# A transformer kernel with a mixture of experts on one core: the way the experts' results are sent, loaded, added and stored at the end of the program

## The reference

```
xn = layernorm(x)
x  = x + attention0(xn) + dense_ffn(xn)          # layer 0
xn = layernorm(x)
x  = x + attention1(xn) @ Wo.T + bo + moe(xn)    # layer 1, masked in blocks of 64

moe: probs = softmax(xf @ gate_w.T); top 2 of 8 experts, weights w normalised
     a token keeps its place at an expert while its rank there is < 320
     out = sum over e of comb[:, e] * (silu(xf@g_e) * (xf@u_e)) @ d_e
```

## Time and profile before

| what | us |
|---|---|
| median of 3 runs (530.13 to 531.07) | 530.15 |
| the profiled execution, its own time | 527.27 |
| its span, first to last instruction | 524.9 |
| PE busy of it | 452.6 |
| DVE busy of it | 400.5 |
| ACT busy of it | 330.0 |
| POOL busy of it | 262.3 |

### The profile page before, as it was taken

How to read it: one execution, slowest core, us unless ns; L and a number is a source line. 1 busy time by engine, 2 the same in 40 slices (tenths; PEclk the granted TensorE clock), 3 DMA queues, 4 the chain that set the end, 5 groups by cost and what they waited for, 6 DMA issues and landing times.

```text
span 524.9 us, 9470 instructions
## 1 busy us (share of the span) xinstructions
PE 452.6 (86%) x3442; PEld 175.6 (33%) x3442; DVE 400.5 (76%) x562; ACT 330.0 (63%) x434; POOL 262.3 (50%) x499
## 2 busy tenths in 40 slices
PE   3555989999999999999989888988999999999850
PEld 1201123324332443244324322321345545455510
DVE  4599889986998699969986987898887777633204
ACT  2201677775777677866785777767856665767550
POOL 6781075723535383788377757873202323253250
PEclk9855899999999999999999999999999999999995
DMA  3896439525720361545263635464720111010018
GB/s 85 232 235 101 76 125 262 173 113 175 148 105 2 124 64 19 64 145 61 24 71 121 79 34 68 142 76 63 88 65 29 46 44 51 11 43 25 16 61 213
DMA packets 143742, 48.27 MB, mean 92 GB/s; under 512 B 109890, under 2 KB 139090, under 8 KB 142866
## 3 DMA queue, kind: packets, MB, share of 16 engines
q1 hardware_dynamic: 141394, 42.93, 39.2%
q0 software_dynamic: 2304, 4.76, 2.7%
HBM read 22.81 MB, written 23.14 MB: 88 GB/s over the span
## 4 chain that ended last, share of the span: by engine, by line
PE 52%; DVE 18%; issue 9%; ACT 9%; SPq 6%; DMA 4%; POOL 1%; POOLq 0%; ACTq 0%; DVEq 0%
PE ps L779 13%; DVE mx L1147 12%; PE ps L763 9%; PE ps L748 7%; ACT PT L992 5%; SPq L446 4%; PE ps L828 4%; PE ps L820 3%; PE ps L709 2%; PE ps L821 2%; PE ps L803 2%; PE ps L843 2%; PE ps L840 2%; PE ps L804 2%; DMA h_all<-y_tokens 1%
## 5 line engine op out<-in xcount | busy, mean ns | idle before, releaser
L1147 DVE TENSOR_REDUCE mx<-ps 128x2 f32<-128x1024 f32 x256 | 307.6, 1221 | 58.6 <-PE ps L748 55.1
L992 ACT ACTIVATE PT<-ps 128x1024 f32<-128x1024 f32 x256 | 258.8, 1025 | 108.2 <-PE ps L763 101.7
L779 PE MATMUL ps<-PT,Vp 128*32 128x512 f32 x1024 | 137.2, 608 | 4.5 <-ACT PT L992 4.4
L748 PE MATMUL ps<-KO,QO 48*128 48x512 bf16 (+1 forms) x512 | 103.9, 404 | 33.8 <-ACT PT L992 15.7
L763 PE MATMUL ps<-QO,KO 59*128 59x512 bf16 x512 | 99.8, 388 | 1.8 <-DVE mx L1147 1.7
L536 POOL DMA_INDIRECT y_tokens<-expert_io,meta x40 | 38.5, 963 | 70.9 <-ACT expert_io L1027 48.1
L763 PEld LDWEIGHTS ps<-QO,KO 59*128 59x128 bf16 x512 | 24.5, 93 | 137.9 <-issue 74.6
L1169 DVE SCALAR_TENSOR_TENSOR th<-th,ps 128x320 f32<-128x320 f32 (+1 forms) x56 | 25.5, 455 | 32.0 <-ACT th L1012 31.6
L748 PEld LDWEIGHTS ps<-KO,QO 48*128 48x128 bf16 (+1 forms) x512 | 25.5, 95 | 63.5 <-ACT PT L992 29.6
L525 POOL DMA_INDIRECT x_places<-xe,place_i x32 | 31.9, 996 | 20.4 <-ACT PT L992 14.6
L561 POOL CAST mp<-mx 128x32 bf16<-128x32 f32 x16 | 3.4, 213 | 72.9 <-DVE mx L1147 69.0
(11 more groups left out here) (166 smaller groups left out, 485.9 us busy)
## 6 DMA issues: line engine op xcount, KB each, us to landing
z<-part SPq DMA_DIRECT2D x16, 384.0 KB, 2.6
z<-part SPq DMA_DIRECT2D x16, 256.0 KB, 3.0
QO<-z SPq DMA_DIRECT2D x64, 48.0 KB
KO<-z SPq DMA_DIRECT2D x64, 48.0 KB
x_places<-expert_io SPq DMA_DIRECT2D x2, 1300.0 KB, 7.2
expert_io<-x_places SPq DMA_DIRECT2D x8, 320.0 KB, 3.7
QO<-z SPq DMA_DIRECT2D x6, 384.0 KB
KO<-z SPq DMA_DIRECT2D x6, 384.0 KB
```

The lines of the kernel that those rows point to most:

```text
L748: mm = pe.matmul(ps[:, 2 * pair + half, :], rows_of(QO[u % 3], half, 2 * s + jj, rows, (qt, qt + 1)), rows_of(KO[u % 3], half, 2 * s + jj, ...
L779: last = pe.matmul(ps[32 * g:32 * g + 32, PV_BANK, :], Vp[u % 2][:, k, head(s, g), :], PT[:, (2 * t + g % 2) % 4, g // 2, :], start=(s % 2 ...
L992: act.activation(PT[:, e % 4], ps[:, 2 * pair:2 * pair + 2, :], ACT.Exp).then_inc(exp_done, 1)
L1147: dve.tensor_reduce(mx[:, a, qt, col:col + 5:4], ps[:, 2 * pair:2 * pair + 2, :], AX_X, ALU.max, negate=True).then_inc(max_read, 1)
```

## The change

Five things are edited. `send_results` keeps its waits on the exponentials only for experts 0 to 2. The rows of `y_tokens` within a sequence are numbered p * 4 + t in place of t * 128 + p (`dest_0`), so that a partition's four tokens are 2 KB in a row. The loads are one pair for each sequence (eight of 256 KB), issued and stored in the order 0, 2, 1, 3 (`ARRIVALS`), each sequence with semaphores of its own. GpSimd adds the results of sequences 0 and 1, behind its last send; VectorE those of 2 and 3, and the projection of unit 7 after them. The last copy into `o_T` is made in two halves, of tiles 0 and 1 and of tiles 2 and 3, and the last projection goes to PV_BANK, tiles 0 and 1 after the first half.

```diff
@@ -234,9 +234,9 @@
         expert_ps = sem("expert_ps")
         y_copied = sem("y_copied")
         y_sent = [sem(f"y_sent{i}") for i in range(2)]
-        y_in = [sem(f"y_in{i}") for i in range(2)]
-        first_added = sem("first_added")
-        result = sem("result")
+        y_in = [sem(f"y_in{b}") for b in range(B)]
+        first_added = [sem(f"first_added{b}") for b in range(B)]
+        result = [sem(f"result{b}") for b in range(B)]
         logit_ps = sem("logit_ps")
         lg_max = sem("lg_max")
         lg_ready = sem("lg_ready")
@@ -376,24 +376,27 @@
             for e in range(E):
                 sp.dma_start(meta[:, e], src[:, e, :, D:ROW]).then_inc(meta_in, 16)
 
-        def results_of(pair):
-
-            t = (Vp[0][:].rearrange("p k h f -> p (k h f)"), h_all[:])[pair]
-            return t[:, 0:4 * NT * D].rearrange("p (k b t d) -> p k b t d", k=2, b=2, d=D)
-
-        def load_results(sp, pair):
-            if pair == 0:
+        def results_of(b):
+
+            t = (Vp[0][:].rearrange("p k h f -> p (k h f)"), h_all[:])[b // 2]
+            return t[:, 0:4 * NT * D].rearrange("p (b k t d) -> p b k t d", k=2, b=2, d=D)[:, b % 2]
+
+
+        ARRIVALS = (0, 2, 1, 3)
+
+        def load_results(sp, b):
+            if b == ARRIVALS[0]:
                 sp.wait_ge(y_sent[0], 16 * JE * (E // 2))
                 sp.wait_ge(y_sent[1], 16 * JE * (E // 2))
                 sp.wait_ge(pv_done, SLOTS_U * (U - 1))
             for k in range(2):
-                first = k * T + 2 * pair * S
-                src = y_tokens[first:first + 2 * S].rearrange("(b t p) d -> p b t d", b=2, p=P)
-                sp.dma_start(results_of(pair)[:, k], src).then_inc(y_in[pair], 16)
+                first = k * T + b * S
+                src = y_tokens[first:first + S].rearrange("(p t) d -> p t d", p=P)
+                sp.dma_start(results_of(b)[:, k], src).then_inc(y_in[b], 16)
 
         def store(sp, b):
             if b < B - 1:
-                sp.wait_ge(result, b + 1)
+                sp.wait_ge(result[b], 1)
             else:
                 sp.wait_ge(unit_done, U)
             sp.dma_start(out[b].rearrange("(t p) d -> p t d", p=P), out_tile(B + b)[:]).then_inc(stored, 16)
@@ -531,8 +534,9 @@
                 pool.wait_ge(meta_in, 16 * E)
             pool.wait_ge(y_copied, e + 1)
             for j in range(JE):
-
-                pool.wait_ge(exp_done, 2 * result_slot(e) + 2 + j)
+                if e < 3:
+
+                    pool.wait_ge(exp_done, 2 * result_slot(e) + 2 + j)
                 pool.indirect_dma_start(out=y_tokens[:], out_offset=bass.IndirectOffsetOnAxis(
                     ap=meta[:].bitcast(I32)[:, e, j, 0:1], axis=0), in_=y_sb[e % 2][:, j, :],
                     in_offset=None).then_inc(y_sent[e % 2], 16)
@@ -829,7 +833,7 @@
                                      ed[:, e, i, :], start=(i == 0), stop=(i == EB - 1))
             last.then_inc(expert_ps, 1)
 
-        def out_mms(pe, u, tiles):
+        def out_mms(pe, u, tiles, bank):
             L = layer(u)
             if tiles[0] == 0:
                 pe.wait_ge(onT_ready, u + 1)
@@ -837,10 +841,10 @@
                     pe.wait_ge(h_ready[0], GATES_U * (u + 1))
             for t in tiles:
                 tok = slice(t * P, (t + 1) * P)
-                last = pe.matmul(ps[:, SIDE, tok], o_T[:, tok], w_proj[L][:], start=True, stop=(L == 1))
+                last = pe.matmul(ps[:, bank, tok], o_T[:, tok], w_proj[L][:], start=True, stop=(L == 1))
                 if L == 0:
                     for i in range(HB):
-                        last = pe.matmul(ps[:, SIDE, tok], h0_T[:, i, tok], wd[:, i, :], start=False,
+                        last = pe.matmul(ps[:, bank, tok], h0_T[:, i, tok], wd[:, i, :], start=False,
                                          stop=(i == HB - 1))
             if tiles[-1] == NT - 1:
                 last.then_inc(y_ps, 1)
@@ -887,7 +891,7 @@
                     pe.wait_ge(qk_f_ready, 2 * p + 2)
                 max_transposes(pe, u, 1)
             if slot == 6 and u >= 1:
-                out_mms(pe, w, (2, 3))
+                out_mms(pe, w, (2, 3), SIDE)
             if slot == 7 and p < U and layer(p) == 1:
                 pe.wait_ge(unit_done, u)
                 rank_mms(pe, p)
@@ -941,7 +945,7 @@
                     value_mms(pe, SLOTS_U * u + slot - 1)
                 if slot == 6 and u >= 1:
                     pe.wait_ge(mT_ready, 2 * u + 2)
-                    out_mms(pe, u - 1, (0, 1))
+                    out_mms(pe, u - 1, (0, 1), SIDE)
                 score_mms(pe, u, slot, 1)
                 if maxima:
                     max_mms(pe, maxima[1])
@@ -962,8 +966,10 @@
             pe.wait_ge(on_ready, 2 * u + 1)
             out_transposes(pe, u, 1)
             normalized_transposes(pe, u)
-            pe.wait_ge(onT_ready, u + 1)
-            out_mms(pe, u, (0, 1, 2, 3))
+
+            out_mms(pe, u, (0, 1), PV_BANK)
+            pe.wait_ge(onT_ready, u + 2)
+            out_mms(pe, u, (2, 3), PV_BANK)
 
 
 
@@ -1089,7 +1095,12 @@
 
         def last_scalar(act):
             output_copy(act, U - 1, 1)
-            onT_copy(act, U - 1)
+            act.wait_ge(onT_ps, U)
+            act.wait_ge(y_ps, U - 1)
+            dst = o_T[:].rearrange("p (t c) -> p c t", c=H)
+            src = ps[:, SIDE, :].rearrange("p (c t) -> p c t", c=H)
+            for t in (slice(0, 16), slice(16, 32)):
+                act.copy(dst[:, :, t], src[:, :, t]).then_inc(onT_ready, 1)
 
 
 
@@ -1185,25 +1196,25 @@
             dve.scalar_tensor_tensor(out=dst, in0=t, scalar=0.5, in1=up, op0=ALU.mult,
                                      op1=ALU.mult).then_inc(h_ready[L], 1)
 
-        def residual(dve, u):
+        def residual(dve, u, bank):
             dve.wait_ge(y_ps, u + 1)
             dve.wait_ge(base_ready, u + 1)
             if u == U - 1:
-                dve.wait_ge(result, B)
-            dve.tensor_tensor(out_tile(u)[:], ps[:, SIDE, :].rearrange("p (t d) -> p t d", d=D), out_tile(u)[:],
+                dve.wait_ge(result[B - 1], 1)
+            dve.tensor_tensor(out_tile(u)[:], ps[:, bank, :].rearrange("p (t d) -> p t d", d=D), out_tile(u)[:],
                               ALU.add).then_inc(unit_done, 1)
 
-        def add_results(dve, b):
+        def add_results(eng, b):
 
             tile = out_tile(B + b)
-            dve.wait_ge(y_in[b // 2], 32)
+            eng.wait_ge(y_in[b], 32)
             if b < B - 1:
-                dve.wait_ge(unit_done, B + b + 1)
+                eng.wait_ge(unit_done, B + b + 1)
             else:
-                dve.wait_ge(base_ready, U)
-            dve.tensor_tensor(tile[:], tile[:], results_of(b // 2)[:, 0, b % 2], ALU.add).then_inc(first_added, 1)
-            dve.wait_ge(first_added, b + 1)
-            dve.tensor_tensor(tile[:], tile[:], results_of(b // 2)[:, 1, b % 2], ALU.add).then_inc(result, 1)
+                eng.wait_ge(base_ready, U)
+            eng.tensor_tensor(tile[:], tile[:], results_of(b)[:, 0], ALU.add).then_inc(first_added[b], 1)
+            eng.wait_ge(first_added[b], 1)
+            eng.tensor_tensor(tile[:], tile[:], results_of(b)[:, 1], ALU.add).then_inc(result[b], 1)
 
         def read_logits(dve, u):
             b = seq(u)
@@ -1225,7 +1236,7 @@
                 if slot == 2 and u >= 1:
                     normalize_out(dve, w, 1)
                 if slot == 7 and u >= 1:
-                    residual(dve, w)
+                    residual(dve, w, SIDE)
                 if slot == 8 and f < U:
                     statistics(dve, f)
                 if slot == 9 and n < U:
@@ -1244,9 +1255,9 @@
 
         def last_vector(dve):
             normalize_out(dve, U - 1, 1)
-            for b in range(B):
+            for b in (2, 3):
                 add_results(dve, b)
-            residual(dve, U - 1)
+            residual(dve, U - 1, PV_BANK)
 
 
 
@@ -1316,7 +1327,8 @@
 
             pool.iota(place_base[:], pattern=[[0, NT], [CAP, 2], [PLACES, E]], base=-1, channel_multiplier=0,
                       allow_small_or_imprecise_dtypes=True).then_inc(consts, 1)
-            pool.iota(dest_0[:], pattern=[[P, NT], [T, 2]], base=0, channel_multiplier=1,
+
+            pool.iota(dest_0[:], pattern=[[1, NT], [T, 2]], base=0, channel_multiplier=NT,
                       allow_small_or_imprecise_dtypes=True).then_inc(consts, 1)
             pool.iota(dump_0[:], pattern=[[P, NT], [T, 2]], base=N_PLACES, channel_multiplier=1,
                       allow_small_or_imprecise_dtypes=True).then_inc(consts, 1)
@@ -1405,9 +1417,9 @@
                 sp.dma_start(dst, src).then_inc(loaded, 16)
             for u in range(U):
                 sync_unit(sp, u)
-            for pair in range(2):
-                load_results(sp, pair)
-            for b in range(B):
+            for b in ARRIVALS:
+                load_results(sp, b)
+            for b in ARRIVALS:
                 store(sp, b)
```

(2 more changed lines are left out.)

## The result

| | before | changed |
|---|---|---|
| median of 10 runs each, side by side | 531.04 us | 529.61 us |
| ratio, 95% interval | | 0.9973 (0.9962 to 0.9984) |
| span of the profiled execution | 524.9 us | 528.1 us |
| the profiled execution's own time | 527.27 us | 530.12 us |

The change made the kernel faster by 1.4 us (0.9 to 2.0), not by 5.7: 529.6 lies outside 522.1 to 525.9. Compared once more later, the ratio was 0.9947 (0.9930 to 0.9965), 2.8 us. That too is less than half of the forecast.

A forecast was written before the change was run, and what follows sets the result against it. The end was taken as bound by an exchange through DRAM: send, land, load, add, store. Residual start 515.75 + 0.70 + 2.72 gave a span of 519.2, 5.7 us under 524.9; median 530.15 - 5.7 = 524.4 us, range 522.1 to 525.9.

The forecast's parts named there:

- step 2: Loads at the end: eight with 2 KB packets at about 395 GB/s, 2.10 MB in 5.3 us, last landed at 512.1.
- step 4: Adds after the loads: VectorE's four done at 513.7, GpSimd's second pair at 513.6; without contention the span ends at 517.2.
- Sends: Experts 6 and 7's sends without the waits: last send at 503.34, first load issued 3.45 us earlier, at 505.61.
- My third case: Final loads gain nothing from 2 KB rows: last landing 515.15 at worst, span ends at 520.4, median 525.6; chance 0.16.
- Projection in halves: Last projection after two half copies: ends at 513.5 in place of 513.97, the residual not before about 513.6.
- store and closing 2.72 us: Kernel's end: time from the end of VectorE's projection addition to the end of the span, taken over from before.
- Adds that meet: VectorE and GpSimd adds delaying each other: two meetings at 1.0 each, 2.0 us, so the residual starts at 515.75.
- the end of that hold at 13.67: Earlier row at 13 us: GpSimd could have held VectorE's subtraction until about 13.67, one third through its operation.

The follow-up runs named there:

- the second trace: The changed kernel run once more with no edit, against the kernel before: ratio 0.9947 (0.9930 to 0.9965), 25.64 us from expert 7's copy to the end.

## Why the prediction was wrong, step by step

Two steps of the sum failed: the loads were taken as too fast (step 2), and the closing of GpSimd's program stood nowhere in it (step 4).

1. **Sends: right, to the hundredth.** 3.45 us, forecast and measured, and without them the change loses (1.0019). The run with this edit alone is at 0.9935.
2. **Loads: the term that was mis-sized, 2.5 us.** "At 395 GB/s 2.10 MB take 5.3 us": the packet time is right (84 ns for each 2 KB packet in the trace, worked out 83), and the rate was reached with four loads, but not held with eight. 9.0 us for 6.5. The price of cutting four loads into eight was taken as SyncE's issue time alone; that was a term without a row. The Trainium skill ("DMA: Bandwidth & Descriptors", "Specifications") has transfers at line rate from 512 bytes on; the runs don't agree: 389 to 412 GB/s with 2 KB packets in four loads against 288 with 512 bytes. My third case had a landing nearly as late, 9.5 us after the first issue, for another reason.
3. **Projection in halves: hidden, as said**, behind the late loads. It ended 2.9 us before it was used, at half clock (2.07 us for 1.24). When the clock falls earlier, as in the second trace, the chain in front of it is 3.5 us late and it does limit; the prediction had its slack at the clock of one trace.
4. **GpSimd's adds: their closing work was missing, 2.1 us.** The sum ended them at 513.6 and set "store and closing 2.72 us" behind VectorE's last addition, with a row of a program in which GpSimd had been done for 14 us. Its own closing DRAIN, 5.96 us, was in the trace of before, between 507.75 and 513.71. The chain of before names a piece of it (`502.70 1.26 POOLq L52`), but no view that I read shows how long it lasts. This is the mechanism that was missing. By the forecast's own times (last add ended at 513.6, residual at 515.75) it would have stood out by 0.6 us only, an estimate; it became 2.1 because the last adds of GpSimd ended 0.7 us before the residual started, and not 2.15. From its last add on GpSimd needs 6.0 us, VectorE's last addition with its store and SyncE's closing 3.2 (522.52 to 525.75): what GpSimd does must end 2.8 us before that addition starts. In the second trace of the changed kernel it ended 2.2 before, and 0.5 us stood out.
5. **Adds that meet: right in kind, 0.94 measured for 1.0 taken, but once and not twice**, since late landings set the adds of sequences 2 and 1 apart. A second meeting, of sequences 0 and 2, cost 0.13. The residual started 2.51 after the last landing, 1.1 less than summed. That an add of two SBUF inputs waits for the whole of GpSimd's add is what the Trainium skill says ("SBUF — State Buffer", "Who interferes with whom"); for two adds the runs agree: in each meeting VectorE's ended 0.54 to 0.55 us after GpSimd's. For the GpSimd operation of the earlier trace rows, with an eighth of the data, the hold was shorter: VectorE's ended 0.20 after it. The prediction put the end of that hold at 13.67 and called it a third of the way through the operation; 13.67 is over half of the way from 13.15 to 14.10.

Together: 2.5 - 1.1 + 2.1 = 3.5 us, the difference of 22.6 and 26.05. Of the 2.3 us that the trace gained, the timed runs show 1.4 in one comparison and 2.8 in the other; what parts these two is open.

## What to carry to other kernels

Add up each engine's program to its very end, closing included: work given to an idle engine is not free if it makes it the last one to close, and here GpSimd had to be through 2.8 us before the chain's last addition. Where a change bundles edits, one of them can carry the gain and the others spend it: the freed sends alone are at 0.9935, the whole change at 0.9947 and 0.9973, and the change with its adds left on VectorE, the first pair pulled into a wait, at 0.9883. And a rate taken from a transfer in few pieces need not hold for the same bytes in twice as many.

## What the runs showed of the hardware

- GpSimd's DRAIN at the end of the program takes 5.96 to 5.98 us in all 14 traces, behind an indirect DMA, an add, a memset, or a wait alone.
- Eight loads of 256 KB fall to 223 to 299 GB/s in the lowest microsecond of their middle, four of 512 KB hold 389 to 412, both with 2 KB packets; the four start slowly (117 GB/s in their first microsecond), as do those of before with 512-byte packets.
- VectorE's add of two SBUF inputs, when GpSimd's add runs first, ends 0.54 to 0.55 us after it: 0.82 to 1.64 us in place of 0.69; when VectorE's runs first, GpSimd's takes up to 1.71 in place of 1.26.
- TensorE's granted clock fell to half at 501.6 to 518.0 us, in some executions before the last value matmuls (the second trace of the changed kernel, 502.7), in others after the projection (all adds on VectorE, 516.4).
